# Two-layer transformer on one core: the second layer's weights turned in 32x32 blocks on VectorE in place of TensorE turns, with a new order of the first layer

## What is computed

```python
h = layernorm(x) * (1 + ca) + sa;  x = x + ga * attention(h)
h = layernorm(x) * (1 + cb) + sb;  x = x + gb * feed_forward(h)
```

```python
h = silu(x @ w1.T * s1) * (x @ w2.T * s2)     # w1, w2: 1024 x 256
h = gelu(h @ h1.T * t1);  h = gelu(h @ h2.T * t2)   # h1, h2: 1024 x 1024
out = h @ w3.T * s3                            # w3: 256 x 1024
```

## Time and profile before

| | us |
|---|---|
| median of 3 runs | 2099.02 (2095.13 to 2100.33) |
| the profiled execution | 2097.95 |
| its span, first to last instruction | 2096.0 |
| TensorE busy | 1958.4 (93%) |
| VectorE busy | 1282.6 (61%) |
| ScalarE busy | 987.2 (47%) |
| GpSimd busy | 519.8 (25%) |

### The profile page before, as it was taken

How to read it: one execution, slowest core, us unless ns; L and a number is a source line. 1 busy time by engine, 2 the same in 40 slices (tenths; PEclk the granted TensorE clock), 3 DMA queues, 4 the chain that set the end, 5 groups by cost and what they waited for, 6 DMA issues and landing times.

```text
span 2096.0 us, 43330 instructions
## 1 busy us (share of the span) xinstructions
PE 1958.4 (93%) x17769; PEld 1471.8 (70%) x17769; DVE 1282.6 (61%) x2370; ACT 987.2 (47%) x1382; POOL 519.8 (25%) x670
## 2 busy tenths in 40 slices
PE   6898989999999987687999999999999999999988
PEld 4566657566666654344778878888787788778887
DVE  5446575756666545556666576566666676675433
ACT  2566555666565653142444444543535434443421
POOL 2325342434434334010211112112202102111111
PEclk8799999999999999798999999999999999999999
DMA  6011211111210003001100000000000000000000
GB/s 184 7 47 60 69 51 62 52 54 54 98 44 31 14 4 131 11 1 65 52 6 24 1 6 24 6 6 19 6 6 19 6 23 2 6 14 6 2 13 7
DMA packets 60693, 67.78 MB, mean 32 GB/s; under 512 B 12281, under 2 KB 49105, under 8 KB 59857
## 3 DMA queue, kind: packets, MB, share of 16 engines
q1 hardware_dynamic: 59664, 64.97, 9.7%
q10 hardware_dynamic: 832, 0.01, 0.0%
HBM read 44.94 MB, written 20.03 MB: 31 GB/s over the span
## 4 chain that ended last, share of the span: by engine, by line
PE 82%; DVE 7%; ACT 5%; issue 2%; POOL 2%; SPq 0%; DMA 0%; DVEq 0%; ACTq 0%; POOLq 0%
PE ps L1979 29%; PE ps L1914 4%; PE ps L1926 4%; PE ps L1883 4%; PE ps L1084 4%; PE ps L1942 3%; PE ps L2016 3%; PE ps L989 3%; PE ps L1136 3%; PE ps L1114 3%; PE ps L1029 2%; PE ps L1047 2%; PE ps L1059 2%; PE ps L1009 2%; PE ps L1033 2%
## 5 line engine op out<-in xcount | busy, mean ns | idle before, releaser
L1837 ACT ACTIVATE b_acts_exact<-ps,c_s 128x256 f32<-128x256 f32 x256 | 107.5, 471 | 366.4 <-PE ps L1979 366.1
L457 POOL TENSOR_SCALAR_AFFINE_SELECT a_probs<-a_probs 128x512 f32<-128x512 f32 (+1 forms) x224 | 162.8, 741 | 438.9 <-ACT a_probs L869 314.4
L1979 PE MATMUL ps<-b_acts,b_h2T 128*128 128x256 f32 x2048 | 262.6, 286 | 1.4 <-DVE b_acts L1751 1.4
L1979 PE MATMUL ps<-b_acts,b_h1T 128*128 128x256 f32 x2048 | 261.0, 286 | 2.2 <-POOL b_acts L1607 1.4
L1979 PEld LDWEIGHTS ps<-b_acts,b_h1T 128*128 128x128 f32 x2048 | 249.4, 191 | 18.6 <-issue 15.0
L1979 PEld LDWEIGHTS ps<-b_acts,b_h2T 128*128 128x128 f32 x2048 | 249.8, 191 | 15.1 <-issue 10.0
L1599 POOL TENSOR_SCALAR_AFFINE_SELECT b_work<-b_work 128x512 f32<-128x512 f32 x128 | 81.7, 650 | 647.4 <-ACT b_work L1801 647.3
L869 ACT ACTIVATE a_probs<-ps 128x2048 f32<-128x2048 f32 (+1 forms) x96 | 153.3, 1597 | 124.5 <-DVEq L711 100.7
L1801 ACT ACTIVATE b_work<-ps 128x2048 f32<-128x2048 f32 (+1 forms) x96 | 153.2, 1596 | 95.0 <-PE ps L1926 94.6
L1672 DVE TENSOR_REDUCE c_nat<-ps 128x4 f32<-128x2048 f32 (+3 forms) x128 | 188.0, 1490 | 3.3
L1750 DVE CAST b_acts<-b_acts_exact 128x512 fp32r<-128x512 f32 x128 | 55.0, 429 | 207.2 <-ACT b_acts_exact L1837 207.0
(11 more groups left out here) (243 smaller groups left out, 3724.5 us busy)
## 6 DMA issues: line engine op xcount, KB each, us to landing
a_raw_next<-in_L_ffn_h_w SPq DMA_DIRECT2D x32, 256.0 KB, 3.0
turned_h<-a_staged SPq DMA_DIRECT2D x32, 256.0 KB, 2.2
a_x<-in_L_attn_x SPq DMA_DIRECT2D x8, 512.0 KB, 4.4
x_mid<-a_x SPq DMA_DIRECT2D x16, 256.0 KB, 2.1
c_x<-x_mid SPq DMA_DIRECT2D x8, 512.0 KB, 3.9
b_h1T<-turned_h SPq DMA_DIRECT2D x1, 4096.0 KB, 16.9
b_h2T<-turned_h SPq DMA_DIRECT2D x1, 4096.0 KB, 14.0
out<-c_x SPq DMA_DIRECT2D x16, 256.0 KB, 2.2
```

What stands on the lines that cost most here:

```text
L457: return nc.gpsimd.affine_select(out=z, in_=z, compare_op=ALU.is_ge, fill=0.0, base=0, pattern=[[0, blocks_n], [1, cols]], channel_multipl ...
L1837: ins = nc.scalar.activation(dst[:, j], here[:, j * HALF:(j + 1) * HALF], ACT.Gelu, scale=s12[:, 2 + (name == "h2"), 2 * i + j:2 * i + j + 1])
L1979: ins = nc.tensor.matmul(dst, view(w[:, m, k]), view(src[:, k, i]), start=(k == 0 and i == 0), stop=(k == nk - 1 and i == 1))
```

## The change

- `load` places the half chunk by many small transfers. The 128 rows of a tile are split in four bands of 32 (p) and its 128 columns in four of 32 (j); the piece (p, j) goes to partitions 32j and up, at columns 32p. Chunks of h1, h2 and w3 take 16 transfers a half, each of 32 partitions by 4 pieces of 128 bytes; chunks of w1 and w2 take 8 of twice that size.
- With the bands in place, turning each 32x32 block by itself gives the turned half. VectorE does that with one transpose of 128x512 from `raw_next` to `staged`, right behind the low-bit check. TensorE's `turn_weights` and ScalarE's copy are gone, and `wt` takes no bank of m0/m1.
- The second norm's four instructions (line 734) take 1/std as a broadcast tensor operand.
- `BODY0`, `START` and `TURN` are new: the same steps in another order, `wt` at other places.

```diff
-wv.3.0+1 lv.3.2+1 wv.3.1+1 win.0.0 lh.3+1 lv.0.0 wh.3+1 tk.1 lin.0.1 turn.1+1 turn.3+1 fold.1 wm.1.0 wt.1 out.0+1 pair.1 out.1+1 again.1 lin.1.0
...
+turn.0 mod-1 again.0-1 wt.5 lin.0.0-1 lv.3.2 wh.3 v.1-1 tq.1-1 win.0.0-1 lh.3 stats-2 tk.1-1 lv.0.0-1 turn.2 lin.0.1-1 turn.1 wt.6 turn.3 fold.1-1
...
         def load(i, half):
             name, m, r = CHUNKS[i]
-            w = weight[name]
-            if r == 1:
-                sp.dma_start(raw_next[half][:], w[m * P:(m + 1) * P, 512 * half:512 * half + 512]).then_inc(raw_loaded[half], 16)
...
+            for j in range(4):
+                place = raw_next[half][R * j:R * j + R].rearrange("a (k p c) -> a k p c", p=4, c=R)
+                if r == 1:
+                    part = weight[name][m * P:m * P + P, 512 * half:512 * half + 512].rearrange("(p a) (k j c) -> j p a k c", a=R, j=4, c=R)
+                    for p in range(4):
+                        sp.dma_start(place[:, :, p], part[j, p]).then_inc(raw_loaded[half], 16)
+                else:
+                    for q in range(2):
+                        row = (m * r + 2 * half + q) * P
+                        part = weight[name][row:row + P, :].rearrange("(p a) (k j c) -> j a k p c", a=R, j=4, c=R)
+                        sp.dma_start(place[:, 2 * q:2 * q + 2], part[j]).then_inc(raw_loaded[half], 16)
...
                 nc.vector.scalar_tensor_tensor(lows[:].bitcast(I32), raw_next[half][:].bitcast(I32), LOW_BITS, lows[:].bitcast(I32),
                                                ALU.bitwise_and, ALU.bitwise_or).then_inc(w_checked, 1)
+                nth = 2 * b + half
+                if nth >= 2:
+                    dve.wait_ge(w_placed[nth % 2], 16 * (nth // 2))
+                nc.vector.transpose(staged[nth % 2][:], raw_next[half][:]).then_inc(w_staged, 1)
...
-                        nc.vector.tensor_scalar(xn[:, t], x[:, b % XR, t], meanvar[:, 1, t, 0:1], rstd[:, 2, t:t + 1], ALU.subtract,
-                                                ALU.mult).then_inc(xn_ready, 1)
+                        nc.vector.scalar_tensor_tensor(xn[:, t], x[:, b % XR, t], meanvar[:, 1, t, 0:1], rstd[:, 2, t:t + 1].broadcast_to([P, D]),
+                                                       ALU.subtract, ALU.mult).then_inc(xn_ready, 1)
```

More of the change, by code:

```diff
@@ L587, in run @@
                 half = step[2]
-                dve.wait_ge(raw_loaded[half], 16 * (b + 1))
+                dve.wait_ge(raw_loaded[half], 16 * sum(16 if r == 1 else 8 for _, _, r in CHUNKS[0:b + 1]))
                 if b + half:
@@ L801, in run @@
                 nc.scalar.activation(cS_next, cT_next, ACT.Silu).then_inc(next_silu, 1)
[L802 to L809, removed]
             elif name == "rows":
@@ L1138, in feed @@
             ins.then_inc(full_sem, 1)
[L1140 to L1146, removed]
         def modulate_next(step):
@@ L1169, in run @@
             name = step[0]
-            if name == "wt":
-                turn_weights(step)
-            elif name == "mod":
+            if name == "mod":
                 modulate_next(step)
@@ L1229 @@
 START = """
[L1230 to L1245, removed]
+0:stats.0 0:norm.0 0:wturn.0.0 0:mod0.0 0:hT.0.0 0:hT.0.1 0:rows.0.0 0:rms.0 0:qk.0.0 0:qk.0.1 0:masks.0 0:qk.0.2 0:qk.0.3 0:wturn.0.1 0:tq.0 0:tk.0
@@ new lines @@
+0:fold.0 0:wm.0.0 0:wturn.0.2 0:v.0.0 0:pair.0 0:mod.0 0:again.0 0:lin.0.0 0:win.0.0 0:v.0.1 0:tq.1 0:lin.0.1 0:tk.1 0:win.0.1 0:wt.0.0 0:fold.1
+0:xg.0 0:wm.1.0 0:wv.0.0 0:wt.0.1 0:wv.0.1 0:lv.0.0 0:rows.0.1 0:pair.1 0:wh.0 0:again.1 0:tq.2 0:lin.1.0 0:lv.0.1 0:stats.1 0:tk.2 0:fold.2 0:wt.1.0
+0:win.1.0 0:lin.1.1 0:norm.1 0:wm.2.0 0:hT.1.0 0:lv.0.2 0:wv.1.0 0:hT.1.1 0:pair.2 0:rms.1 0:lh.0 0:wt.1.1 0:lv.1.0 0:again.2 0:win.1.1 0:tq.3 0:tk.3
+0:win.2.0 0:qk.1.0 0:lv.1.1 0:wt.2.0 0:wv.1.1 0:lin.2.0 0:fold.3 0:qk.1.1 0:wm.3.0 0:qk.1.2 0:lv.1.2 0:wh.1 0:lin.2.1 0:wt.2.1 0:qk.1.3 0:pair.3
@@ L1246 @@
+0:lin.8.1 0:lh.7 0:lv.8.0 0:fold.9 0:wm.9.0 0:wv.7.1 0:turn.1.0 0:turn.1.2 0:turn.1.1 0:wh.7 0:pair.9 0:turn.1.3 0:wv.8.0 0:stats.3 0:again.9 0:tq.10
+0:lin.9.0 0:out.1.0 0:out.1.1 0:win.8.1 0:lv.8.1 0:tk.10 0:lin.9.1 0:fold.10 0:lv.8.2 0:wm.10.0 0:wv.8.1 0:xT.1.0 0:lh.8 0:xg.2 0:pair.10 0:wh.8
+0:wt.7.1 0:xT.1.1 0:wt.8.0 0:lv.9.0
 """
 TURN = """
-0:lin.26.0 0:r.5.0 0:r.5.1 0:tq.27 0:lin.26.1 0:wv.25.0 0:tk.27 0:win.26.0 0:norm.7 0:lh.25 0:lv.26.0 0:kk.5.0 0:hT.7.0 0:wv.25.1 0:lv.26.1 0:hT.7.1
@@ L1270 @@
[L1270 to L1272 removed]
+0:win.25.0 0:lv.25.1 0:again.26 0:win.25.1 0:tq.27 0:lv.25.2 0:lin.26.0 0:tk.27 0:wv.25.0 0:lin.26.1 0:norm.7 0:lh.25 0:fold.27 0:lv.26.0 0:wv.25.1
@@ new lines @@
+0:wm.27.0 0:lv.26.1 0:r.5.0 0:hT.7.0 0:hT.7.1 0:rms.7 0:wh.25 0:pair.27 0:qk.7.0 0:qk.7.1 0:win.26.0 0:qk.7.2 0:qk.7.3 0:lv.26.2 0:win.26.1 0:v.7.0
+0:again.27 0:lin.27.0 0:wv.26.0 0:wv.26.1 0:tq.28 0:win.27.0 0:v.7.1 0:tk.28 0:lin.27.1 0:fold.28 0:r.5.1 0:wm.28.0 0:kk.5.0 0:lh.26 0:lv.27.0
+0:pair.28 0:lv.27.1 0:kk.5.1 0:lin.28.0 0:again.28 0:wh.26 0:wv.27.0 0:lv.27.2 0:win.27.1 0:tq.29 0:last.5.0 0:win.28.0 0:last.5.1 0:wv.27.1
+0:lin.28.1 0:lh.27 0:tk.29 0:lv.28.0 0:win.28.1 0:wh.27 0:fold.29 0:wm.29.0 0:wv.28.0 0:turn.6.0 0:wv.28.1 0:turn.6.2 0:pair.29 0:again.29 0:tq.30
```

67 lines of the change are left out of this document (34 added, 33 removed).

## The result

| | us |
|---|---|
| before, median of 4 runs | 2098.05 (2095.13 to 2100.33) |
| after, median | 2067.89 |
| after / before | 0.9854, 95% interval 0.9836 to 0.9872 |
| profiled execution of after | 2068.71, span 2066.8 |

The change makes the kernel 1.46% faster, 30 us. Of four runs of after one took 5381.97 us; it was disturbed and is left out.

What follows compares the result with a forecast made beforehand. TensorE was taken to set the pace, except in one stretch of a pass that VectorE bounds. Terms -18.6, -8.5, +4, -6, -4 and -3 summed to -36 us, from 2097.95 to 2062 us; range 2038 to 2090.

Steps and rivals of the forecast that it cites:

- TensorE's turns, -18.6: Layer passes: removing 44 turns of 0.59 us from TensorE, 5 of 7 counted, gains 18.6 us, between 13 and 26.
- ScalarE's copies and the bank, 0: `wt` steps: dropping 44 copies of 0.587 us and freeing their m0/m1 bank gains 0, between 0 and -3 us.
- +4 elsewhere: 38 transposes where VectorE has slack, each delaying something due in one of six cases: +4 us, between 0 and +13.
- The page's rival for them: Each VectorE transpose takes four 128x128 blocks one after the other, 1.24 us; total 2069; no chance given.
- my first rival: VectorE bounds more places in a pass; half the turns' gain and all the order's go: 2089 us, 15% chance.
- Place A, -8.5: Output product to shift columns: one check and one transpose replace two checks; 1.5 us a pass, -8.5 us in all.
- The second norm, 0 (-1 to +2): Second norm's VectorE instructions with two tensor operands instead of one: cost 0, between -1 and +2 us in all.
- SP's loads, 0: SP's queue: 640 small-load issues for 44, one in 0.5 us, covered by 3 us: cost 0, bounds 0 and +5.
- the slow rival: SP issues over 0.75 us each fill the pass and VectorE waits for `raw_next`; 2240 us at 1.0 us; 8% chance.
- START -6: Kernel start: a value projection and `mod` fill TensorE's waits at the first quad; -6 us, between +5 and -15.
- TURN -4: Between the layers: `xg.7` some 30 steps earlier, products `r.6` and `kk.6` cover the first norm; -4 us, +4 to -10.
- The clock, -3: In the passes: a smaller TensorE gap behind the output product may keep the clock up; -3 us, between +3 and -12.

## Why the prediction came out right, point by point

The sum was -36 and the result -30, inside the range, but not by its own steps.

- **TensorE's turns, -18.6: the step that failed.** "Where TensorE is the bound it is all gain", I wrote, and counted 5 of 7. On the old list they are worth 4.1 us, not 18.6 (and 3.3 for three quarters of them, with the norm's form left alone). TensorE was busy 95% there, yet the turns stood where it would have waited: a turn's place in the list has to be priced, not TensorE's share. Half of the sign for this was in the trace: three of seven turns stood among or shortly ahead of the gaps of the earlier trace rows, and I took off only one or two.
- **ScalarE's copies and the bank, 0: mis-sized.** I wrote that the bank "now stays with the other turns" and counted nothing. On the new list the last quarter of a turn with its bank and copy is worth 30 us. The two errors have opposite signs, and the sum survived them; that is luck.
- **The transposes.** Duration 0.70 against 0.69, right. +4 elsewhere: 1.9 us between the medians without and with them, none of it in a pass; right within what can be told. The page's rival for them (four blocks one after the other, 1.24 us) falls with L602's row: 0.70 / 4 = 0.18 us a 128x128 in float32, where the Trainium skill, "VectorE: DVE Perf Modes", The three transpose paths, gives 311 ns in bf16. On the old list they cost 7 us together with the small loads (2092.9 to 2099.9), nearer to my first rival.
- **Place A, -8.5.** The picture was right, a gap under 1.6 and a clock over 0.83: 0.45 and 1.00. The size was not: TensorE's idle in a pass fell by 0.9 us, not 1.5, with the rest of the pass counted in.
- **The second norm, 0 (-1 to +2).** The mean rose from the earlier trace rows's 576 ns to 679; by medians in one order the form costs 97 ns. The group in after:

```profile
L742 DVE SCALAR_TENSOR_TENSOR a_xn<-a_x,a_meanvar,a_rstd 128x256 f32<-128x256 f32 x32 | 19.9, 679 | 9.0 <-POOL a_rstd L457 9.0
```

  No effect in a pass; at most the 4.8 us of the run with the old form in all.
- **SP's loads, 0.** Right: 0.57 us each in a row where I took 0.5, 9.2 us for a half and 1.8 to land; VectorE never waits for one, and large loads gain 3 us in all between the medians, none of it in a pass and not clear of noise. SP had 14.5 us a pass to spare. The threshold was sharper than I saw: twice the issues, and the slow rival is there. The rule of the Trainium skill, "DMA: Bandwidth & Descriptors", Rules for kernel authors, that small transfers are mostly overhead holds in SP's time of issue; the fixed 2 us, one after the other, that I worked out from it doesn't: 16 loads landed in 11 us. (The page fits those 2 us to transfers issued from GpSimd; these are issued from SP.)
- **START -6:** -8.1 on the new passes, +3.3 on the old ones. Right for this change, but no number of START's own. **TURN -4:** 1.2 us between batch 5 and the end, within its bounds. `xg.7` left the chain, but the second layer's first turn came at 782.43, 30 us earlier and not the 36 that would have made 775:

```profile
782.43 5.40 PE ps L1874 x16
```

- **The clock, -3.** The half clock behind place A is gone, 3.4 us of full speed in a pass. Part of its price shows in before's trace behind place A, where a turn of 0.66 us and a product of 0.63 at full clock take 1.11 and 1.06:

```profile
484.30 1.11 PE L1009 MATMUL ps<-c_identr,a_shift_cols 128*128 128x128 f32 x4
485.35 1.06 PE L1084 MATMUL ps<-a_probs,c_va 128*17 128x256 f32 x8
```

  What it is worth in a whole pass stays open: with turns TensorE is busy 91.41 us of a pass in the new tables at clock 1.00, and 91.65 in the old ones at 0.96. At the turn, from batch 5's output product to batch 7's, the clock is lower in after, 0.90 over 246 us against before's 0.93 over 232, though the new `TURN` puts somewhat other steps there; from batch 5's to the end it is 0.98 in both. Before, then after:

```profile
645.37:877.75 232.38, 193.75 (x1955) 125.28 (x1954) 131.75 (x232) 106.93 (x136) 72.40 (x89) 0.93 0.10 38
...
617.37:863.01 245.64, 205.12 (x2014) 127.97 (x2010) 139.66 (x243) 110.45 (x138) 75.51 (x93) 0.90 0.12 39
```

Of the rivals, "the order takes back" came true for the old tables with blocks (+3 us), not for after. The passes near 90 (90.9), the 44 transposes, the 576 smaller loads at 0.43 us and VectorE not waiting for `raw_next` were all as forecast; the 64 loads of twice the size took 0.61 us, over the 0.35 to 0.5 that I gave.

**Open:** how much of what makes the new tables slow with turns is the bank, beyond the 1.4 us a pass that the traces show, and how much the copy in ScalarE's list; and whether tables searched anew for turns on TensorE would reach 2068 too. Neither was tried.

## What to carry to other kernels

In a kernel whose engines walk one hand-made list, an operation's time on the bounding engine is not its price: look at what stands right behind it, and if the engine waits there, removing the operation buys the wait. Here a step's last quarter with its copy and its place in a pool of two PSUM banks was worth more than the rest of its time on TensorE, but only with an order made for it, so try mechanism and order together before rejecting either alone. The many small transfers were free here while the issuing queue had idle time in each round; add up the issues at their spacing in a row, not at the duration of one, and stop before that sum reaches the round.
